# A layer of attention, experts and a state space on one core: how the routing weights of two mixtures reach the 128 partitions

## What is computed

```python
router_logits = sigmoid(x @ gate_w + gate_b)                  # 16 experts
expert_values, expert_indices = top_k(router_logits, k=2)
expert_values = expert_values / sum(expert_values)
hg = einsum('bsd,edi->bsei', x, experts_wg)                   # 64 inner features for each expert
hu = einsum('bsd,edi->bsei', x, experts_wu)
all_outputs = einsum('bsei,eid->bsed', silu(hg) * hu, experts_wd)
# the two selected experts of a token, weighted by expert_values
return x + mlp(x, shared_wg, shared_wu, shared_wd) + expert_weighted
```

## Time and profile before

| | |
|---|---|
| median of three runs | 878.74 us |
| the profiled execution: its time / its span | 878.15 us / 876.3 us |
| busy: TensorE, VectorE, ScalarE, GpSimd | 89 %, 55 %, 49 %, 49 % of the span |
| granted TensorE clock, mean | 0.957 of full speed |
| DMA traffic | 8.14 MB, 9 GB/s over the span |

### The profile page before, as it was taken

The page is one execution under the profiler, slowest core; times in us unless marked ns, Lnnn a source line. Parts: engine busy times, 40 slices in busy tenths (PEclk is TensorE's granted clock), DMA queues, the critical chain, the costliest instruction groups (busy, mean ns, idle before and its releaser), DMA issues. The chain is left out here.

```text
span 876.3 us, 14873 instructions
## 1 busy us (share of the span) xinstructions
PE 779.5 (89%) x6024; PEld 523.5 (60%) x6024; DVE 478.3 (55%) x718; ACT 432.4 (49%) x564; POOL 433.7 (49%) x310
## 2 busy tenths in 40 slices
PE   1689999999999999999999998989899676579998
PEld 1455555555555556565555555968788432558887
DVE  6653554454554455455545511766575685666552
ACT  3344445555544544554554451566565560276543
POOL 2044755674575566558556675143344262133443
PEclk9889999999999999999999999999999785789999
DMA  2000000000000000000000002300000000000000
GB/s 60 7 1 1 7 2 1 7 1 1 8 1 1 7 1 1 8 1 1 1 2 25 1 1 76 87 1 1 1 1 1 0 1 0 1 0 13 7 8 25
DMA packets 18963, 8.14 MB, mean 9 GB/s; under 512 B 7952, under 2 KB 18768, under 8 KB 18896
## 3 DMA queue, kind: packets, MB, share of 16 engines
q1 hardware_dynamic: 18896, 7.20, 3.2%
HBM read 6.15 MB, written 1.05 MB: 8 GB/s over the span
## 5 line engine op out<-in xcount | busy, mean ns | idle before, releaser
L476 DVE TENSOR_REDUCE at_half_max<-at_ring 128x2 f32<-128x1024 f32 (+1 forms) x192 | 177.2, 955 | 120.8 <-PE at_ring L571 104.7
L359 POOL TENSOR_TENSOR all_x<-all_x,at_probs 128x1024 f32<-128x1024 f32 (+3 forms) x128 | 220.4, 1722 | 40.5 <-ACT at_probs L432 25.7
L432 ACT ACTIVATE at_probs<-at_ring 128x1024 f32<-128x1024 f32 x144 | 147.1, 1023 | 145.8 <-PE at_ring L605 127.3
L359 POOL TENSOR_TENSOR all_x<-at_probs 128x768 f32<-128x768 f32 (+1 forms) x32 | 66.9, 2092 | 165.1 <-ACT at_probs L432 164.9
L1128 POOL TENSOR_TENSOR m_prod<-m_gate,m_wb_copy 128x512 f32<-128x512 f32 x64 | 82.4, 1292 | 124.5 <-ACT m_gate L956 124.5
L623 PE MATMUL at_out<-at_probs,at_k_nat 128*64 128x512 f32 (+3 forms) x768 | 140.3, 494 | 1.1 <-DVE a_attn_t L497 0.9
L596 PE MATMUL at_ring<-at_qh,at_kh 64*128 64x512 f32 (+3 forms) x384 | 77.7, 401 | 21.2 <-DVE at_m_rows L488 21.0
L623 PEld LDWEIGHTS at_out<-at_probs,at_k_nat 128*64 128x64 f32 x768 | 49.2, 136 | 66.1 <-issue 59.3
L853 PEld LDWEIGHTS m_acc<-rest_wd,m_hid 128*128 128x128 f32 x576 | 76.6, 195 | 6.2
L956 ACT ACTIVATE m_gate<-m_g 128x512 f32<-128x512 f32 x72 | 43.1, 598 | 73.1 <-PE m_g L845 72.4
L564 PE MATMUL at_ring<-at_kh,at_qh 64*128 64x512 f32 (+3 forms) x384 | 74.8, 395 | 4.0 <-DVE at_half_max L476 2.4
(11 more groups left out here) (224 smaller groups left out, 1408.9 us busy)
## 6 DMA issues: line engine op xcount, KB each, us to landing
all_x<-in_L_attn_a_x SPq DMA_DIRECT2D x8, 256.0 KB, 4.0
at_w_raw<-in_L_attn_a_W_qk SPq DMA_DIRECT2D x8, 128.0 KB, 2.5
out<-all_x SPq DMA_DIRECT2D x4, 256.0 KB, 2.3
a_room<-in_L_attn_a_W_out SPq DMA_DIRECT2D x1, 512.0 KB, 4.0
m_raw_wg<-in_L_ffn_experts_wg SPq DMA_DIRECT2D x1, 512.0 KB, 4.7
m_raw_wu<-in_L_ffn_experts_wu SPq DMA_DIRECT2D x1, 512.0 KB, 4.3
rest_wd<-in_L_ffn_experts_wd SPq DMA_DIRECT2D x1, 512.0 KB, 4.2
rest_w_in<-in_L_attn_b_W_in SPq DMA_DIRECT2D x1, 256.0 KB, 4.3
```

Source lines behind the costliest of these rows:

```text
L359: return pool.tensor_tensor(sums[:, :, a * P:b * P], left, right, ALU.add)
L432: act.activation(probs[:, :, slot * BANK:(slot + 1) * BANK], pair("S", unit, slot)[:, :, :], ACT.Exp, scale=BETA).then_inc(exp_done, 1)
L476: last = dve.reduce_max(half_max[:, :, i, int(a > 0)], pair("M", unit, m)[:, :, at:at + (b - a) * P], AX.X)
```

## The change

The selection matrix, the spreading matmul, its PSUM bank and the ScalarE copy go. The weights of a group are copied once from PSUM to SBUF as 16 rows of 512 numbers of 32 bits (2 KB each), in a buffer that holds one group, and VectorE's `w_low` goes. SyncE's queue then issues two DMAs for each step: each reads one row (one partition) 64 times and writes it to 64 partitions. The spread weights have four buffers, each with its own semaphore. `w_high` of group n > 0 waits until all DMAs of the group before have landed.

```diff
 RING = 2
 BUFS = 3
+SPREAD = 4
@@ PREPARE
-               w_high=-2, w_low=-3)
+               w_high=-2)
@@ mixture
-        wb = [s.sb(f"wb_copy{r}", [P, BANK]) for r in range(2)]
+        wb = [s.sb(f"wb{r}", [P, BANK]) for r in range(SPREAD)]
+        wb_loaded = [s.sem(f"wb_loaded{r}") for r in range(SPREAD)]
@@ TensorE
-                def spread(g):
...
-                    pe.matmul(wb_ps[:, :], f.sel[:, st, :], f.wt[:, cols(n)],
-                              start=True, stop=True).then_inc(wb_ready, 1)
...
-                    if g > 0 and ahead(g + 1):
-                        spread(g + 1)
@@ ScalarE
-                    act.activation(wb[(LAST * n + st) % 2][:, :], wb_ps[:, :], ACT.Copy).then_inc(wb_copied, 1)
...
-                            act.wait_ge(sel_made, 5)
-                            act.activation(f.sel[:, :, :], sel[:, :, :], ACT.Copy).then_inc(const_done, 1)
...
                         act.wait_ge(wt_ready, n + 1)
-                        act.activation(f.wt[0:EXPERTS, cols(n)], misc[1][0:EXPERTS, :], ACT.Copy)\
-                           .then_inc(wt_high, 1)
+                        if n:
+                            last = LAST * n - 1
+                            for r in range(SPREAD):
+                                act.wait_ge(wb_loaded[r], 32 * ((last - r) // SPREAD + 1))
+                        act.activation(f.wt[:, :], misc[1][0:EXPERTS, :], ACT.Copy).then_inc(wt_done, 1)
@@ VectorE
-                        dve.tensor_tensor(f.wt[32:32 + EXPERTS, cols(n)], misc[1][0:EXPERTS, :],
-                                          f.wt[0:EXPERTS, cols(n)].bitcast(FP32), ALU.subtract).then_inc(wt_low, 1)
@@ GpSimd
-                        pool.wait_ge(wb_copied, LAST * n + st + 1)
+                        q = LAST * n + st
+                        pool.wait_ge(wb_loaded[q % SPREAD], 32 * (q // SPREAD + 1))
...
@@ SyncE
+                    def spread(n, st):
+
+                        q = LAST * n + st
+                        wait(sp, weighted, q - SPREAD + 1)
+                        for e in range(2):
+                            sp.dma_start(wb[q % SPREAD][e * INTER:(e + 1) * INTER, :],
+                                         f.wt[2 * st + e:2 * st + e + 1, :].unsqueeze(1).to_broadcast([1, INTER, BANK]))\
+                              .then_inc(wb_loaded[q % SPREAD], 16)
...
+                    for n in range(GROUPS + 1):
+                        if n < GROUPS:
+                            sp.wait_ge(wt_done, n + 1)
+                            for st in range(SPREAD):
+                                spread(n, st)
+                        if n and store is not None:
+                            sp.wait_ge(acc_used, n)
+                            sp.dma_start(grp(store, n - 1), grp(k.x, n - 1)).then_inc(stored, 16)
+                        for st in range(SPREAD, LAST if n < GROUPS else 0):
+                            spread(n, st)
@@ rest
-    f.sel = r.sb("sel", [P, EXPERTS // 2, P], F32R)
-    f.wt = r.sb("wt", [P, TOKENS], F32R)
+    f.wt = r.sb("wt", [EXPERTS, BANK])
```

More of the change, by code:

```diff
@@ L780, in mixture @@
     with Scope(nc, tag) as s:
-        g_ps, u_ps, wb_ps, acc, misc = s.ps("g", RING), s.ps("u", RING), s.ps("wb"), s.ps("acc"), s.ps("misc", 2)
+        g_ps, u_ps, acc, misc = s.ps("g", RING), s.ps("u", RING), s.ps("acc"), s.ps("misc", 2)
         src_ps = [g_ps[0], g_ps[1], u_ps[0], u_ps[1]]
@@ L785, in mixture @@
         hid = [s.sb(f"hid{r}", [P, BANK]) for r in range(BUFS)]
-        wb = [s.sb(f"wb_copy{r}", [P, BANK]) for r in range(2)]
-        wb_copied = s.sem("wb_copied")
-        g_ready, u_ready, wb_ready = s.sem("g_ready"), s.sem("u_ready"), s.sem("wb_ready")
+        wb = [s.sb(f"wb{r}", [P, BANK]) for r in range(SPREAD)]
+        wb_loaded = [s.sem(f"wb_loaded{r}") for r in range(SPREAD)]
+        g_ready, u_ready = s.sem("g_ready"), s.sem("u_ready")
         gated, weighted = s.sem("gated"), s.sem("weighted")
@@ L801, in mixture @@
         logit_ready, scored, nat_ready, nat_read = [s.sem(n) for n in ("logit_ready", "scored", "nat_ready", "nat_read")]
-        route_step, w_ready, wt_ready, wt_high, wt_low = [
-            s.sem(n) for n in ("route_step", "w_ready", "wt_ready", "wt_high", "wt_low")]
+        route_step, w_ready, wt_ready, wt_done = [
+            s.sem(n) for n in ("route_step", "w_ready", "wt_ready", "wt_done")]
         if weights:
@@ L806, in mixture @@
             gate_raw = s.sb("gate_raw", [P, EXPERTS])
-            sel = s.sb("sel", [P, EXPERTS // 2, P])
             iota_i = s.sb("iota_i", full, I32)
-            loaded, split, padded, low_split, iota_made, sel_made, const_done = [
-                s.sem(n) for n in ("loaded", "split", "padded", "low_split", "iota_made", "sel_made", "const_done")]
+            loaded, split, padded, low_split, iota_made = [
+                s.sem(n) for n in ("loaded", "split", "padded", "low_split", "iota_made")]
         def grp(t, n):
@@ L816, in cols @@
             return slice(n * BANK, (n + 1) * BANK)
-        def ahead(g):
-            return g < NSTEPS and g % STEPS < LAST
         def interleave(pieces, emit, step, tiles=False):
@@ L891, in step @@
                         emit("turn_w", 0, "first")
-                        spread(0)
-                        spread(1)
                         emit("logits", 1, "first")
@@ L919, in emit @@
                         pe.wait_ge(before.low, n + 1)
-                        wait(pe, wt_low, n)
+                        wait(pe, wt_done, n)
                         o = misc[1][0:EXPERTS, :]
@@ L956, in step @@
                     act.activation(gate[g % BUFS][:, :], g_ps[g % RING][:, :], ACT.Silu).then_inc(gated, 1)
-                    if ahead(g + 1):
-                        copy_weights(g + 1)
                 def emit(piece, n, kind):
@@ L974, in emit @@
                             act.wait_ge(loaded, 16 * 8)
-                            act.wait_ge(padded, 4)
+                            act.wait_ge(padded, 3)
                             act.activation(f.gate_hi[:, :], gate_raw[:, :], ACT.Copy).then_inc(split, 1)
@@ L985, in emit @@
                            .then_inc(scored, 1)
-                        if weights and n == 0:
-                            act.wait_ge(sel_made, 5)
-                            act.activation(f.sel[:, :, :], sel[:, :, :], ACT.Copy).then_inc(const_done, 1)
                     elif piece == "w_high":
                         act.wait_ge(wt_ready, n + 1)
-                        if weights and n == 0:
-                            act.wait_ge(padded, 4)
-                        act.activation(f.wt[0:EXPERTS, cols(n)], misc[1][0:EXPERTS, :], ACT.Copy)\
-                           .then_inc(wt_high, 1)
+                        if n:
[3 more added lines that the diff above has]
+                        act.activation(f.wt[:, :], misc[1][0:EXPERTS, :], ACT.Copy).then_inc(wt_done, 1)
                 interleave(("square", "root", "high", "sigmoid", "w_high"), emit, step)
@@ L1084, in emit @@
                         dve.tensor_tensor(w[:, :, :], w1[:, :, :], w2[:, :, :], ALU.add).then_inc(w_ready, 1)
-                    elif piece == "w_low":
-                        dve.wait_ge(wt_high, n + 1)
-                        dve.tensor_tensor(f.wt[32:32 + EXPERTS, cols(n)], misc[1][0:EXPERTS, :],
-                                          f.wt[0:EXPERTS, cols(n)].bitcast(FP32), ALU.subtract).then_inc(wt_low, 1)
                     elif piece == "add_up":
@@ L1094, in emit @@
                                           acc[:, :].rearrange("p (t d) -> p t d", t=PER), ALU.add).then_inc(acc_used, 1)
-                interleave(("source", "centre", "variance", "norm", "low", "route1", "route2", "route3", "w_low", "add_up"),
+                interleave(("source", "centre", "variance", "norm", "low", "route1", "route2", "route3", "add_up"),
                            emit, step)
@@ L1103, in _ @@
                         pool.memset(raw[n][:, EXPERTS + 1, :], 0.0).then_inc(padded, 1)
-                    pool.memset(f.wt[:, :].bitcast(FP32), 0.0).then_inc(padded, 1)
+                    pool.wait_ge(padded, 2)
+                    pool.memset(f.wd[INTER:P, EXPERTS // 2, :], 0.0).then_inc(padded, 1)
                     pool.wait_ge(padded, 3)
-                    pool.memset(f.wd[INTER:P, EXPERTS // 2, :], 0.0).then_inc(padded, 1)
-                    pool.wait_ge(padded, 4)
                     pool.iota(iota_i[:, :, :], pattern=[[0, PER], [1, EXPERTS]], base=0, channel_multiplier=0)\
                         .then_inc(iota_made, 1)
[L1111 to L1118, removed]
                 def step(g):
@@ L1137, in _ @@
                 interleave(("residual",), emit, step)
-            if weights or store is not None:
+            if True:
                 @block.sync
                 def _(sp):
+                    def spread(n, st):
[5 more added lines that the diff above has]
```

(6 more changed lines are left out.)

6 lines of the change are left out of this document (1 added, 5 removed).

## The result

The changed kernel takes 1257.35 us (four runs, 1256.38 to 1257.50) against 878.56 us before: ratio 1.431, 95 % interval 1.429 to 1.433. It is 379 us slower. The forecast was 1385 us, in a range from 1030 to 1650 us.

The account below looks back on a forecast made before the run. TensorE was taken to bound the kernel before, the single-partition DMA reads after. 878.15 - 202.4 (old stretches) + 16 (gaps) + 2 (half clock) = 693.8 us, plus 691 us for 64 pairs: 1385 us, range 1030 to 1650 us.

Parts of the forecast that it names:

- TensorE bounds the kernel, and the spreading matmul is on its path: Both mixtures before the change: TensorE sets the time; removing 64 spreading matmuls of 0.23 us saves 14.7 us.
- the rival: Weight DMAs in both mixtures: reads stay hidden behind the steps, kernel faster at 864 to 868 us; chance 0.16.
- One partition supplies the 16 engines one way's rate: Weight DMAs: a pair's reads go one after another through one engine's way, 10.8 up to 14.5 us; chance 0.70.
- T: Time of one step's pair of weight DMAs, 262,144 B, taken as 10.8 us; 64 of them give 691 us.
- The gap of a group: Start of each group, waiting for the last landing before: copy plus DMA latency, 2.0 us, eight times, 16 us.
- Only the last store is on the end ... Nothing charged: Stores in SyncE's queue in m2: one waits behind the next group's first four pairs; cost taken as nothing.
- The half clock costs 2 us at the ends: Last 16 down matmuls of each mixture: 4.0 us at half clock, 1 us more than now, 2 us for both.
- SyncE's queue waiting for `m_prod`: Sign in the profile after: SyncE's queue waits for GpSimd's products rather than issuing without pause; no size given.
- The repetition on one engine: Rival for the weight DMAs: one engine carries both of a pair, same 10.8 us and 1385 us; no separate chance.
- Each partition a way of its own: Rival for the weight DMAs: a pair's two rows don't share a way, 5.4 us a pair, 1040 us; chance 0.10.
- Worse than one engine's way: Rival for the weight DMAs: 16 engines' requests on one partition disturb each other, over 1650 us; chance 0.03.
- The port figure of the Trainium skill: Reads of a pair's rows: both leave through one port at some 27 GB/s, about 9.6 us a pair, about 1310 us.

Follow-up runs that it names:

- many rows: Changed kernel with each DMA reading 64 different partitions of a constant tile instead of one row 64 times, routing weights left out: 867.10 us.
- the copies at 32 and 64: Changed kernel with the 16 rows also written from partition 32, or from 64, and read there by each pair's second DMA: 1266.37 us and 1030.39 us.

## Why the prediction was right

- *TensorE bounds the kernel, and the spreading matmul is on its path:* right. Without it and without DMAs the kernel takes 868 us; the rival said 864 to 868.
- *One partition supplies the 16 engines one way's rate:* right in its mechanism, shown by the runs with many rows, with the copies at 32 and 64 and with the rows in HBM. The term was mis-sized: T was taken as 10.8 us from the 24.3 GB/s of one engine; it is 8.13 us where no gap disturbs it (two buffers for the rows), 32 GB/s. One way gives the 16 engines some 27.7 GB/s (the slices of 1 us above), which would be 9.5 us a pair; the turns from one group of four rows to the next, with two ways at once, bring it down. 64 x 2.67 us = 171 us too much. Its row was also misread: the densest slices of the load are 430 and 420 GB/s, not 389, though slices of 287 and 297 stand beside them; 430 GB/s would have given 9.8 us and 1318 us.
- *The gap of a group:* 2.0 us was too little. With T = 8.13 us, 64 T is 520 us; of the 580.5 us, 60 us are left, of which the stores take 11 (below) and the eight gaps 49, 6 us each. 33 us too little.
- *"Only the last store is on the end ... Nothing charged":* wrong. The three inner stores stand in the same queue as the weights, 4.84 us each in issue, and make their groups 3.4 to 3.8 us longer, 11 us in all. The median landing of the four stores goes from 2.3 to 12.9 us.
- *The half clock costs 2 us at the ends:* half of it shows. The 16 down matmuls after the last product take 3.78 us at a granted clock of 0.50 in m2, near the 4.0 us forecast, and the span goes on 9.3 us from the start of that product instead of 8.4. In m1 they take 2.05 us at 0.96, so nothing shows there. As the first copy comes 0.6 us earlier, the rest of the span grew by 0.2 us only. Over the two stretches the granted clock is 0.67 and 0.66, a mean of parts at 0.50 (584 to 588 us) and at 1.00 (572.5 to 576 us), and TensorE is busy half of the time rather than the quarter forecast; it is not the bound there, since its work hides under T.
- Together: 171 - 33 - 11 = 127 us too much in the two stretches and 1.8 us outside them; the forecast is 128.6 us over the 1256.38 us of the profiled execution.
- *SyncE's queue waiting for `m_prod`:* the wrong sign to look for. It waits for it 5.3 us in all; instead an issue lasts 3.8 us in the first group (16 in 60.35 us), presumably since the queue takes no more until the engines have done some. The dear issues are an effect and not the cause: with many rows seven take 4.34 us.
- *The repetition on one engine:* fell by the DMA share of 7 to 8 tenths. *Each partition a way of its own:* the changed kernel speaks against it, since its pairs already have two partitions, and the run with the copy at 64 rules it out, since there the rows of a pair are two partitions as before and the time falls by 227 us. *Worse than one engine's way:* fell by T = 8.13 us. The port figure of the Trainium skill (SBUF — State Buffer, Door 1: The DMA port swizzle) gave an estimate of 1310 us, nearer than the 1385 from the row; what the estimate leaves out are the turns, at which two ways are read.

## What to carry to other kernels

In these runs a DMA that repeats one SBUF row reads through one way, though all its engines and 64 destination partitions take part: before replacing compute by such DMAs, divide the repeated bytes by some 30 GB/s and compare with a step. If the row has to be repeated, put it in HBM first (32 KB and 1.6 us here) and repeat it from there; that turned 379 us lost into 8 us won. In a profile, DMA engines that are busy at a tenth of their usual GB/s, and DMA issues that take several times 0.47 us, are signs that the engines share a source or a target.

## What was not expected of the hardware

- Rows spread over four or eight ways gave hardly more than over two: over the first group 4.4 us a pair with two, 4.2 with four, 4.3 with eight. Only a second issuing queue went beyond, 79 and 94 GB/s in stretches.
- Two rows that are read in turn overlap for a moment when they lie on different ways: 57 to 80 GB/s in single microseconds, between long parts at 27.7 GB/s.
- Letting the queue run empty once a group cost 5.7 us, nearly three times the 2.0 us of a copy and a DMA's latency.
- 16.8 MB of DMA writes into SBUF beside full engines cost nothing that can be measured: 867.10 us with them, 868.17 us without.
